# A four-layer graph network on one core: destination segments found by comparing neighbouring edges, and the sums by source run in 10 pieces of 250 columns

## What is computed

```
src = src[_o]; dst = dst[_o]             # _o sorts the edges by dst, 400000 edges
out = segment_sum(h[src] * alpha, dst)   # layer 1 (twice): attention, sums by destination
agg = segment_sum(m, row)                # layer 2: messages, sums by source (row = src)
out = x - zeros.at[src].add(msg_s) - zeros.at[dst].add(msg_d)   # layer 3: both
aggregated = segment_sum(transformed, pair_indices[:, 0])       # layer 4: sums by source
x = layernorm(x + layer(x))              # behind each layer
```

## Time and profile before

| | |
|---|---|
| median of three runs | 26084.06 us (26073.52 to 26091.56) |
| the profiled execution, its own time | 26059.39 us |
| span in its profile | 26057.3 us |
| busy: PE, DVE, ACT, POOL | 61%, 62%, 15%, 70% |
| POOL's indirect transfers, its costliest group | 6250 of 952 ns |

### The profile page before, as it was taken

How to read it: one execution, slowest core, us unless ns; L and a number is a source line. 1 busy time by engine, 2 the same in 40 slices (tenths; PEclk the granted TensorE clock), 3 DMA queues, 4 the chain that set the end, 5 groups by cost and what they waited for, 6 DMA issues and landing times. The chain is left out here.

```text
span 26057.3 us, 352712 instructions
## 1 busy us (share of the span) xinstructions
PE 15985.8 (61%) x99055; PEld 11771.6 (45%) x99058; DVE 16265.3 (62%) x41454; ACT 3861.1 (15%) x8407; POOL 18368.4 (70%) x17570
## 2 busy tenths in 40 slices
PE   4200000026666663888884588888888838999993
PEld 3200000015555552666663355554554526777772
DVE  9466666617777771777774366666666654666664
ACT  0000000012222221111110111111111101222220
POOL 0477777767777774777773577777777767888884
PEclk6555555555555555888885688888888967889886
DMA  3111111101111110111112011111111120000002
GB/s 125 48 33 32 33 33 32 32 13 32 31 32 32 31 30 9 25 25 25 25 26 66 16 19 20 20 19 20 20 19 20 20 71 22 25 24 25 25 25 73
DMA packets 1032548, 815.57 MB, mean 31 GB/s; under 512 B 602135, under 2 KB 922911, under 8 KB 1028513
## 3 DMA queue, kind: packets, MB, share of 16 engines
q0 software_dynamic: 561792, 189.30, 5.8%
q1 hardware_dynamic: 366264, 291.81, 4.2%
q10 hardware_dynamic: 104400, 333.49, 3.2%
HBM read 416.39 MB, written 396.80 MB: 31 GB/s over the span
## 5 line engine op out<-in xcount | busy, mean ns | idle before, releaser
L891 POOL DMA_INDIRECT gat_got<-table,gat_idx x6250 | 5951.9, 952 | 1907.4 <-issue 1903.6
L1389 POOL DMA_INDIRECT msgs<-msg_msg,msg_pos x4875 | 5815.2, 1193 | 1550.0 <-issue 1484.7
L1624 POOL DMA_INDIRECT sheaf_got<-table,sheaf_idx x3125 | 3181.5, 1018 | 952.6 <-issue 952.6
L1288 PE MATMUL msg_dps<-msg_dhotq,msg_dleft 128*128 x16500 | 3437.8, 370 | 0.0
L1288 PE MATMUL sheaf_dps<-sheaf_dhotq,sheaf_dleft 128*128 x18000 | 3335.3, 342 | 0.8 <-DVE sheaf_dhotq L1271 0.8
L353 PE MATMUL hist_s_counts<-hist_s_hot_k,hist_s_hot_a 128*98 128x128 bf16 x3125 | 362.8, 314 | 3567.0 <-DVE hist_s_hot_k L306 3567.0
L1197 PE MATMUL place_look_ps<-place_nexts,place_hot_at 98*128 98x128 f32 x5000 | 1635.7, 467 | 1320.9 <-DVE place_same L1102 924.4
L1288 PEld LDWEIGHTS msg_dps<-msg_dhotq,msg_dleft 128*128 x16500 | 1814.8, 114 | 1346.1 <-issue 570.0
L1288 PEld LDWEIGHTS sheaf_dps<-sheaf_dhotq,sheaf_dleft 128*128 x18000 | 1818.9, 102 | 1305.2 <-issue 252.6
L1498 ACT COPY msg_flip<-msg_fps 128x384 f32<-128x384 f32 (+1 forms) x3000 | 1361.7, 494 | 5383.6 <-PE msg_fps L1456 5374.0
L1632 POOL DMA_INDIRECT msgs<-sheaf_msg,sheaf_pos x1625 | 1786.2, 1099 | 519.2 <-issue 519.2
(11 more groups left out here) (468 smaller groups left out, 27861.8 us busy)
## 6 DMA issues: line engine op xcount, KB each, us to landing
gat_got<-table,gat_idx POOLq DMA_INDIRECT x6250
msg_ex<-ex SPq DMA_DIRECT2D x250, 400.0 KB
gat_sums<-gat_acc ACTq DMA_DIRECT2D x125, 675.0 KB, 3.3
msgs<-msg_msg,msg_pos POOLq DMA_INDIRECT x4875
tail_m<-msgs SPq DMA_DIRECT2D x75, 800.0 KB
src_sums<-tail_acc ACTq DMA_DIRECT2D x75, 800.0 KB
gat_sums<-gat_acc ACTq DMA_DIRECT2D x125, 425.0 KB, 2.6
ex<-zeros ACTq DMA_DIRECT2D x25, 2000.0 KB
```

Of the source, the lines that this page charges most:

```text
L891: pool.indirect_dma_start(got[b][:, j, :], None, table, bass.IndirectOffsetOnAxis(idx[b][:, j:j + 1], 0)).then_inc(gathered[b], 16)
L1288: last = pe.matmul(self.acc[:, n, 0:self.BQ], left, hot_q, start=False, stop=False, skip_group_check=True)
L1389: pool.indirect_dma_start(msgs, bass.IndirectOffsetOnAxis(pos[b][:, j:j + 1], 0), msg[b][:, j, :], None).then_inc(scattered[b], 16)
L1624: pool.indirect_dma_start(got[b][:, j, :], None, table3, bass.IndirectOffsetOnAxis(idx[b][:, j:j + 1], 0)).then_inc(gathered[b], 16)
```

## The change

In the first part `find_segments_by_destination` takes the place of `find_segments("d")`. It loads all destinations into SBUF (`dst_all`, 128 x 3125 int32) and, for each partition but the first, the last destination of the partition ahead of it (`ahead`: 127 rows of 4 bytes). `keep_d` is 1 where an edge has the same destination as the edge before it; `fresh` is made from `keep_d`. The rows (start + 1, end) are stored once, in node order, to a small table `segment_rows`, and one indirect gather with the first destination of each partition as index fetches `seg`. There is no `marks_d` any more, and it isn't cleared. `find_segments("s")` stays, without its branch for "d".

In the second part the three calls of `sum_by_source` run `RUNS` = 10 pieces of `LONG` = 250 columns in place of 25 of 100; nothing else in it is changed.

```diff
-    CT = C_S // NCT
+    RUNS = NCT // 5 * 2
+    LONG = C_S // RUNS
...
-    marks = {o: dram(f"marks_{o}", [P * cols_of[o], 2]) for o in ("d", "s")}
+    marks = {"s": dram("marks_s", [P * C_S, 2])}
+    segment_rows = dram("segment_rows", [NR, 2])
...
-                    parts = ((ex32, EXW, C), (ex4, 4, C), (marks["d"], 2, C), (marks["s"], 2, C_S), (msgs, D, C_S),
+                    parts = ((ex32, EXW, C), (ex4, 4, C), (marks["s"], 2, C_S), (msgs, D, C_S),
...
+        def find_segments_by_destination():
...
+                @block.vector
+                def _(dve):
+                    ch = Chain(dve, steps)
+                    dve.memset(ahead[:, :], -1).then_inc(cleared, 1)
...
+                    ch.add(dve.tensor_scalar(mark[:, :, 0], g["start"][:, :], 1.0, None, ALU.add))
+                    dve.tensor_copy(mark[:, :, 1], end[:, :]).then_inc(marked, 1)
...
+                    dve.wait_ge(came, 32)
+                    ch.add(dve.tensor_tensor(keep["d"][:, 1:C], dst_all[:, 1:C], dst_all[:, 0:C - 1], ALU.is_equal))
+                    ch.link(dve.tensor_tensor(keep["d"][:, 0:1], dst_all[:, 0:1], ahead[:, :], ALU.is_equal))
+                    ch.add(dve.tensor_scalar(fresh[:, :], keep["d"][:, :], BIG, -BIG, ALU.mult, ALU.add))
+                    dve.wait_ge(looked, 16)
...
+                @block.sync
+                def _(sp):
+                    sp.dma_start(dst_all[:, :], dst_v).then_inc(came, 16)
+                    sp.wait_ge(cleared, 1)
+                    with nc.allow_non_contiguous_dma(reason="one edge a partition"):
+                        sp.dma_start(ahead[1:P, :], dst_v[0:P - 1, C - 1:C]).then_inc(came, 16)
+                    sp.wait_ge(marked, 1)
+                    sp.dma_start(node_rows(segment_rows), mark[:, :, :]).then_inc(kept, 16)
+
+                @block.gpsimd
+                def _(pool):
+                    pool.wait_ge(came, 32)
+                    pool.wait_ge(kept, 16)
+                    pool.indirect_dma_start(seg[:, :], None, segment_rows, bass.IndirectOffsetOnAxis(dst_all[:, 0:1], 0)
+                                            ).then_inc(looked, 16)
...
-                m = [sb(f"{name}_m{b}", [P, CT, D], F32, ctx) for b in range(2)]
-                acc = [sb(f"{name}_acc{b}", [P, CT, D], F32, ctx) for b in range(2)]
+                m = [sb(f"{name}_m{b}", [P, LONG, D], F32, ctx) for b in range(2)]
+                acc = [sb(f"{name}_acc{b}", [P, LONG, D], F32, ctx) for b in range(2)]
...
-                        sp.dma_start(m[b][:, :, :], msg_v[:, bass.ds(i * CT, CT), :]).then_inc(loaded[b], 16)
-                    run_turns(sp, NCT, body)
+                        sp.dma_start(m[b][:, :, :], msg_v[:, bass.ds(i * LONG, LONG), :]).then_inc(loaded[b], 16)
+                    run_turns(sp, RUNS, body)
...
-            find_segments("d")
+            find_segments_by_destination()
```

More of the change, by code:

```diff
@@ L149, in gnn_kernel @@
     GK = 4
-    assert E == P * C and C % CW == 0 and NCH % 5 == 0 and D == 16 and NP <= P
+    assert E == P * C and C % CW == 0 and NCH % 25 == 0 and C_S % RUNS == 0 and D == 16 and NP <= P
     H1, C1 = L0_gnn_a_src1.shape
@@ L404, in _ @@
                     run_turns(pe, NCH, lambda i, b, turn, first: hist.pe(pe, i, b, turn, first))
+        def find_segments_by_destination():
+            g = order["d"]
+            with ExitStack() as ctx:
+                incl, end = sb("incl_d", [NP, NK], F32, ctx), sb("end_d", [NP, NK], F32, ctx)
+                tmp, zero = sb("tmp_d", [NP, NK], F32, ctx), sb("zero_d", [NP, NK], F32, ctx)
+                mark = sb("mark_d", [NP, NK, 2], F32, ctx)
+                dst_all, ahead = sb("dst_all", [P, C], I32, ctx), sb("dst_ahead", [P, 1], I32, ctx)
+                seg, v = sb("seg_d", [P, 2], F32, ctx), sb("v_d", [P, 8], F32, ctx)
+                ps = ctx.enter_context(nc.psum_tensor("ps_d", [P, 512], F32))
+                steps, totals, offs, marked, kept, came, looked, cleared = (
+                    sem(f"seg_{n}_d") for n in ("steps", "totals", "offs", "marked", "kept", "came", "looked", "cleared"))
+                block = ctx.enter_context(nc.Block())
+                @block.vector
+                def _(dve):
+                    ch = Chain(dve, steps)
+                    dve.memset(ahead[:, :], -1).then_inc(cleared, 1)
+                    ch.link(dve.memset(zero[:, :], 0.0))
+                    dve.tensor_tensor_scan(incl[:, :], cnt[:, :], zero[:, :], 0.0, ALU.add, ALU.add).then_inc(totals, 1)
+                    dve.wait_ge(offs, 1)
+                    ch.add(dve.tensor_scalar(g["has"][:, :], cnt[:, :], 0.0, None, ALU.is_gt))
+                    ch.link(dve.tensor_copy(v[0:NP, 0:1], ps[0:NP, 0:1]))
+                    ch.link(dve.tensor_scalar(end[:, :], incl[:, :], v[0:NP, 0:1], None, ALU.add))
+                    ch.link(dve.tensor_tensor(g["start"][:, :], end[:, :], cnt[:, :], ALU.subtract))
+                    ch.add(dve.tensor_scalar(mark[:, :, 0], g["start"][:, :], 1.0, None, ALU.add))
+                    dve.tensor_copy(mark[:, :, 1], end[:, :]).then_inc(marked, 1)
+                    ch.link(dve.tensor_scalar(tmp[:, :], g["has"][:, :], -FAR, FAR, ALU.mult, ALU.add))
+                    ch.link(dve.tensor_tensor(tmp[:, :], tmp[:, :], g["start"][:, :], ALU.add))
+                    ch.link(dve.tensor_copy(g["put"][:, :], tmp[:, :]))
+                    ch.link(dve.tensor_scalar(tmp[:, :], end[:, :], -1.0, 0.0, ALU.add, ALU.max))
+                    ch.add(dve.tensor_copy(g["take"][:, :], tmp[:, :]))
+                    dve.wait_ge(came, 32)
[3 more added lines that the diff above has]
+                    dve.wait_ge(looked, 16)
+                    a1, b = seg[:, 0:1], seg[:, 1:2]
+                    ch.add(dve.tensor_tensor(v[:, 0:1], a1, first_edge["d"][:, :], ALU.is_le))
+                    ch.add(dve.tensor_tensor(v[:, 1:2], b, last_edge["d"][:, :], ALU.is_le))
+                    ch.add(dve.tensor_tensor(v[:, 2:3], b, last_edge["d"][:, :], ALU.is_ge))
+                    ch.add(dve.tensor_scalar(v[:, 3:4], b, -1.0, None, ALU.add))
+                    ch.link(dve.tensor_scalar(v[:, 4:5], a1, -1.0, None, ALU.add))
+                    ch.add(dve.tensor_tensor(g["whole"][:, :], v[:, 0:1], v[:, 2:3], ALU.mult))
+                    ch.add(dve.tensor_copy(g["fix_get"][:, :], v[:, 3:4]))
+                    ch.add(dve.tensor_copy(g["begins"][:, :], v[:, 4:5]))
+                    ch.link(dve.tensor_tensor(v[:, 5:6], v[:, 0:1], v[:, 1:2], ALU.mult))
+                    ch.link(dve.tensor_scalar(v[:, 6:7], v[:, 5:6], -FAR, FAR, ALU.mult, ALU.add))
+                    ch.link(dve.tensor_tensor(v[:, 7:8], v[:, 6:7], v[:, 3:4], ALU.add))
+                    ch.link(dve.tensor_copy(g["fix_put"][:, :], v[:, 7:8]))
+                @block.tensor
+                def _(pe):
+                    pe.wait_ge(totals, 1)
+                    pe.matmul(ps[0:NP, 0:1], earlier[0:NP, 0:NP], incl[:, NK - 1:NK], start=True, stop=True
+                              ).then_inc(offs, 1)
+                @block.sync
[12 more added lines that the diff above has]
+                                            ).then_inc(looked, 16)
@@ L1539, in body @@
                         for f in range(D):
-                            last = dve.tensor_tensor_scan(acc[b][:, :, f], keep["s"][:, bass.ds(i * CT, CT)], m[b][:, :, f],
-                                                          acc[1 - b][:, CT - 1, f:f + 1], ALU.mult, ALU.add)
+                            last = dve.tensor_tensor_scan(acc[b][:, :, f], keep["s"][:, bass.ds(i * LONG, LONG)], m[b][:, :, f],
+                                                          acc[1 - b][:, LONG - 1, f:f + 1], ALU.mult, ALU.add)
                         last.then_inc(summed, 1)
                         dve.wait_ge(summed, i + 1)
-                    run_turns(dve, NCT, body)
-                    dve.tensor_copy(last_rows[:, :], acc[(NCT - 1) % 2][:, CT - 1, :])
+                    run_turns(dve, RUNS, body)
+                    dve.tensor_copy(last_rows[:, :], acc[(RUNS - 1) % 2][:, LONG - 1, :])
                 @block.scalar
```

12 lines of the change are left out of this document (5 added, 7 removed).

## The result

The changed kernel takes **25827.35 us** (median of 4 runs, 25824.64 to 25833.58), the kernel before 26078.79 us in the same comparison (4 runs, 26070.66 to 26091.56). The ratio is 0.9903, 95% interval 0.9886 to 0.9921: faster by 251 us, or 206 to 297.

What follows compares the result with a forecast made beforehand. POOL's issuing was taken to bound the segments block and `tail2`, DVE then transfers the outer tails; -178 - 2 x 32 + 43 = -199 us, so 26084 - 199 = 25885 us, range 25850 to 25920 (8 in 10: 25822 to 25950).

Steps and rivals of the forecast that it cites:

- Segments, -178: Block finding segments by destination: without POOL's 128 scatters the next block starts at about 879 us, not 1057.3; -178 us.
- the rival in which each takes a round trip: Segments block: 127 small rows not pipelined, 1.7 us each, cost 216 us; sum +16 us; chance 0.02.
- Clearing at nothing: ACT's 25 clearing issues no longer needed, 21.5 us, counted as no gain because ACT issues them beside the histogram.
- `tail1` and `tail3`, -32 each: Sums by source in the two outer tails: ten pieces of 250 columns take 125.7 us in place of 157.96.
- The 118 us: Outer tails: time by the skill's transfer rule, sum 16 us lower; the forecast kept the rows' 385 GB/s instead.
- `tail2`, +43: Middle sum by source, where POOL ends last: gathers stall behind longer bulk transfers, 218 us in place of 175.5.
- about five waiting: Middle tail: POOL can have about five unserved gathers before it must stop, so 5.5 are served a piece.
- -8 if the stretched instructions went too: Middle tail: the lower bound on its forecast change of +43 us; the upper bound was +62.
- Rule and row: Middle tail: engines drain whole packets before changing queues, so gathers wait for whole transfers, 2.5 times as long; basis of +43.
- The gathers don't mind: Rival for the middle tail: POOL can have ten or more waiting, or long rows let them by; -242, 25842 us; chance 0.28.
- The tails gain nothing: Rival for the sums by source: mixed long transfers no faster per byte, outer tails +7 each; -121, 25963 us; chance 0.10.
- slower: Rival for the segments block: the 127 small rows are not pipelined, costing 216 us; sum +16 us; chance 0.02.

## Why the prediction was right, and where it was not

- **Segments, -178: right**, -179.0 by the profile. Its parts were less exact, and errors cancel in it: the load with the small rows behind it was in 7.2 us after the start, where 8.8 were worked out, while POOL's gather starts only at 881.03, 8.3 us after DVE's first operation, since the small store lands late, takes 4.28 us in place of 1, and lets DVE wait 1.43 us. Against the 5.7 us that were worked out for the big load, the 127 rows of 4 bytes and their landing cost some 1.5 us together; the rival in which each takes a round trip is out.
- **Clearing at nothing: wrong by +10.** The step "I cost it at nothing, since ACT issues them beside the histogram" looked at ACT alone. Its rows are also a spacing between big transfers, and what is late is a load of keys on another queue. The runs with the clearing kept and with it split give the 10 us back.
- **`tail1` and `tail3`, -32 each: right**, -31.6 and -31.5, out of errors that cancel: c, DVE's time for a piece, is 10.2 us and not 9.8 (a column costs 2.07 ns between 100 and 250, not the 1.87 of the earlier trace rows and 7), 4 us more in ten pieces, and the waits between pieces are 10.6 us in all, spread over eight pieces with 0.2 to 2.2 each, where four of 3.3 were forecast. The 118 us that the prediction drew for a tail from the Trainium skill (DMA: Bandwidth & Descriptors, section "Anatomy of one DMA") are 8 below the 126.4 measured; the page gives its figures for DMAs that GpSimd issues, and these are SP's and ACT's.
- **`tail2`, +43: wrong, it is -9.** The step that failed is "if POOL can have about five waiting and one slips through between load and store, 5.5 are served a piece". DMA view of the changed kernel within a piece's bulk (20993 to 21001 us), and in the pause behind it, as the earlier trace rows (packets, MB, share):

```profile
q10 hardware_dynamic: 108, 1.73, 50.3%
q1 hardware_dynamic: 105, 1.68, 50.2%
q0 software_dynamic: 74, 0.02, 1.0%
```

```profile
q0 software_dynamic: 208, 0.04, 10.0%
```

In 8.0 us of bulk 74 packets are 2.4 gathers, and in 2.2 us of pause 208 are 6.7. So some 9 are served in a piece of 11.5 us, which is all that POOL issues (11.5 / 1.26). POOL goes on beside the long scans, 0.94 to 0.96 us for each of its instructions in this bulk. The "about five waiting" was too few. Source view of the gathers that were started by 21012.5 us, and what POOL's queue had got through by then:

```profile
L767 POOL DMA_INDIRECT seg_of_d<-dst_sums,take_d x67: 938/961/1407, 20927.6 to 21011.6; - x67
```

```profile
q0 software_dynamic: 1921, 0.38, 2.7%
```

At 32 packets a gather 60 are served, so seven wait, and POOL isn't held up. Twelve wait with five pieces, and no trace shows an end of the room. That the stretched instructions of before showed it was the wrong reading: they go with DVE's scans. The bound "-8 if the stretched instructions went too" is what came, but not for its reason, and some 2 us of it are gathers that are shorter even with nothing beside them.
- **Rule and row.** In the bulk one gather passes for 213 / 2.4 = 89 long rows, 5.6 for each of 16 DMA engines. The Trainium skill (DMA: Bandwidth & Descriptors, section "Queues, rings and completion order") has an engine change queues at whole packets of some 9 to 17 descriptors. The trace agrees that a gather waits for a group of rows, and that the group is dearer with longer rows (3.3 us a gather here, and 7 us with rows of 32 KB: 64 packets in 14 us of bulk with five pieces). But the group is smaller than a whole transfer, 128 rows or 8 for each engine, and gathers that wait hold nobody up as long as there is room for them, of which the rule says nothing; so +43 didn't follow from it.
- **The rivals.** "The gathers don't mind" is what happened; its first ground, room for more than five, holds. That the time came so near its 25842 is in part luck, since it had neither the +10 of the histogram nor the +15 of the third layer, nor the -9 of `tail2`. "The tails gain nothing" and "slower" are out. The forecast's own range, 25850 to 25920, missed.

The terms as measured: -179 + 10.3 - 63.1 - 9 + 9 elsewhere = -232 between the profiled executions. The sum of the forecast missed by +52 in `tail2` and -10 and -9 in what it held for nothing.

## What to carry to other kernels

Work that is taken off an engine nobody waits for also spaces that engine's transfers; look at what shares the DMA engines with them before calling it free. A stretched instruction shows that something held it up, not what: before building a queue model on it, look for a stretch where the supposed cause is stronger and the instruction isn't stretched, and for one where the cause is absent and it is. When a double-buffered stream waits for its own stores, part the way there and back from the rate: a third buffer takes the former, longer pieces both a share of it and the fixed cost of each instruction.

## What the hardware showed that was not expected

- A load and a store stream together ran at 403 GB/s with a DMA share of 0.99 over 41 us beside DVE's full row of scans (three buffers of 250 columns), and at 411 GB/s over 97 us with few scans; 385 had been taken.
- POOL's gather instructions are stretched by DVE's work beside them: up to 3.5 us beside scans of 100 columns with three buffers, every second one 1.9 us beside scans of 500, even with next to no other transfer, hardly beside scans of 250, and not with most scans gone and more transfers. The path stays open.
- The one gather in the block of the segments took POOL 4.28 us and ended 0.1 us after DVE's `fresh`; a later one of 128 rows, in the join behind `tail1`, took 0.99.
- Twelve gathers of POOL were started and not yet served with five pieces, and their instructions were no longer than with hardly any waiting.
- The same gather instruction, with nothing beside it, has a median of 969 ns in the kernels that have `find_segments("d")` and of 956 to 958 in the others (shortest 965 and 938). The cause was not looked for.
